# Reordering the expert loop, spreading the weight folding and pacing the last scatters in a fused graph and mixture-of-experts kernel on Trainium2

## The chip, the cores and the metric

The kernel runs on one core of one Trainium2 chip. The metric is the device time in microseconds (us) of one execution, as the median of several runs. Engines are named as in the profile: PE (TensorE) with PEld (its weight loads), DVE (VectorE), ACT (ScalarE), POOL (GpSimd) and SP (SyncE, which only issues DMAs here). A small `q` behind a name means its sequencer.

## The reference

The input is `x`, 128 graphs of 128 nodes with 128 features, in float32, and a weighted adjacency matrix for each. Four residual layers follow each other:

```
x = x + gnn0(layernorm(x), adj)       # softmax-like attention over neighbours
x = x + ffn0(layernorm(x))            # 30 steps of tanh, silu, layernorm, 128x128 product
x = x + relu(z @ Wa + (adj @ z) @ Wb + bias)     # z = layernorm(x), second graph layer
logits = x @ Wr + br                  # for each of 16384 tokens, 8 experts
top 2 experts, weights w1, w2 from the softmax
out = x + sum_k w_k * (gelu((norm(x)*g_e + b_e) @ W1[e] + b1[e]) @ W2[e] + b2[e])
```

W1[e] is 128x512 and W2[e] 512x128. Only the two chosen experts of a token count.

## The kernel before

The 128 graphs are 16 streams of 8. All engines run their own programs, written out by hand, and meet in semaphores; there is no scheduler. So the order on an engine is the order of the calls in its block, and each wait stands in the code ahead of the instruction that it holds.

**The second graph layer** is a pipeline over `GNN1_SLOTS` steps. In step k stream k is transposed, stream k-1 multiplied, k-2 mixed with its adjacency, k-3 finished on VectorE (`finish_rows`, `row_variances`), k-4 given its logits, k-5 routed (`route`), k-6 ranked (a matmul that counts tokens of each pair of experts), k-7 placed (`find_slots`). Placing gives each token a row in `sorted_rows`, in DRAM. There are 28 pairs of experts, each with a region of its own, and a token with its two weights, its index, its mean and variance is one row of 133 floats. POOL writes the rows by eight indirect DMAs a stream (`scatter`, L538), four ahead of the power operation for a later stream and four behind it. After step 15 there is no such operation, and the last four streams' 32 scatters stand directly one behind the other.

**Folding.** The layer norm's scale and shift of each expert are folded into W1 and its bias, after the pipeline's streams: TensorE sums the columns (`fold_wide`) and adds `b1` by a 1-row matmul (L1206, L1208), VectorE combines (L833). The eight experts go by twos in the last steps, from step 19.

**Between the stages.** VectorE turns the pairs' row counts into tables: which 128 rows (a slab) are to be loaded, and for which two experts (`slab_row`, `slab_exp`). Regions are rounded up to slabs, so SP and ACT fill 29 pieces of padding (`fill`, L376), waiting for `tables_ready`. Then SP copies eight weight matrices and loads the first rows (`load_weights` L423, `load_rows` L416), after `w1_folded`, `pads_in` and `scattered`.

**Experts.** 156 slabs of 128 tokens, each with two experts. The first 12 and the last 12 slabs are unrolled, 132 run in a loop of 12 a turn. Products are numbered o, two a slab. POOL computes the row scales (`scale`, L569) and writes results by an indirect DMA (`store`, L574). VectorE normalizes rows (`normalize`, L896), adds the second bias from `b2_all` by the expert's number, and combines (`finish`, L904, L909). ACT does the GELU (L1022) and copies the transposed rows (L1027). TensorE's order for an even o is:

```python
first_product(i, o)
if o % 2 == 0 and (not end or o < 2 * EACH - 4):
    turn(i, o // 2 + 2)
if not first or o >= 2:
    second_product(i, o - 2, expert_of(i, o - 2))
```

`turn` (L1225) transposes the rows of the slab after next and waits for its `normalize`. `expert_of` (L1221) loads the expert's number from SBUF into a register; `second_product` (L1244) picks its weights by it. `first_product` (L1235) reads one of eight buffers `w1_in_use`, which SP fills again once `hidden_psum` shows that the product of eight before is done.

## Time and profile before

| what | us |
|---|---|
| median of 3 runs (2808.33 to 2822.69) | 2814.98 |
| the profiled execution, its own time | 2804.9 |
| its span, first to last instruction | 2803.1 |
| PE busy in the span | 2489.5 |
| DVE busy | 2075.3 |
| POOL busy | 2029.8 |
| ACT busy | 1809.0 |

The profile is that of one execution, which was 10 us shorter than the median. A busy time is a sum over stages that differ. Where a stage is bound is read from the waits inside it and from the starts of neighbouring instructions. A row names the tile that lies at an address first, so `adjT` and `resid` also stand for the buffers of the expert stage that lie over them.

### The profile page before, as it was taken

The numbers are of one execution on the slowest core, as the hardware profiler recorded it, in microseconds if no ns is written. First come the engines' busy times: TensorE is split into PE (matmuls) and PEld (weight loads), VectorE is DVE, ScalarE is ACT, GpSimd is POOL, SyncE is SP. The second block draws the span as 40 slices with busy tenths as digits, with TensorE's granted clock in tenths as the row PEclk, the third lists the DMA queues.
The fourth block names the chain that finished last, engine by engine and source line by source line (L and its number), as shares of the span: only waits on it lengthen the run. The fifth ranks groups of instructions, "written<-read, shape, count | busy, mean of one in ns | idle before, by whom it ended". The sixth has DMA issues, their size and how long they took to land.

```text
span 2803.1 us, 62675 instructions
## 1 busy us (share of the span) xinstructions
PE 2489.5 (89%) x19950; PEld 2340.0 (83%) x19951; DVE 2075.3 (74%) x5754; ACT 1809.0 (65%) x2185; POOL 2029.8 (72%) x1592
## 2 busy tenths in 40 slices
PE   6839999999999999999999999886588888888887
PEld 5839999999999999999999999882577777777777
DVE  6999999999999999999999998674122222222222
ACT  3779999999999999999999973220222222222222
POOL 5779999999999999999999997775232332323323
PEclk9969999999999999999999999995799999999999
DMA  9000000000000000000000000411433333333332
GB/s 267 35 1 1 0 0 0 0 0 0 0 0 0 0 0 0 0 0 0 0 0 0 0 1 32 132 43 49 141 129 125 123 125 125 127 123 126 123 123 76
DMA packets 123642, 141.98 MB, mean 51 GB/s; under 512 B 14951, under 2 KB 76547, under 8 KB 123553
## 3 DMA queue, kind: packets, MB, share of 16 engines
q1 hardware_dynamic: 112450, 122.86, 13.3%
q0 software_dynamic: 9088, 17.14, 1.9%
q10 hardware_dynamic: 2016, 0.95, 0.1%
q8 instruction: 37, 0.61, 0.1%
q14 instruction: 51, 0.42, 0.0%
HBM read 36.35 MB, written 24.58 MB: 22 GB/s over the span
## 4 chain that ended last, share of the span: by engine, by line
DVE 54%; PE 29%; issue 9%; ACT 4%; another core or an unknown queue 2%; SPq 1%; DMA 0%; DVEq 0%; POOL 0%; POOLq 0%; ACTq 0%
DVE pair_stats L639 23%; DVE state L682 17%; PE psum L1244 12%; PE psum L1235 10%; DVE state L661 6%; PE psum L1072 3%; ACT adjT L1022 3%; PE psum L1062 2%; DVE it_vars L643 1%; DVE x_stats L639 1%; DVE resid L709 1%; DVE state L678 1%; DVE resid L669 0%; PE psum L1208 0%
## 5 line engine op out<-in xcount | busy, mean ns | idle before, releaser
L1072 PEld LDWEIGHTS psum<-w_ffn,turned 128*128 128x128 f32 x7680 | 1010.0, 192 | 36.1
L1072 PE MATMUL psum<-w_ffn,turned 128*128 128x128 f32 x7680 | 1013.6, 275 | 0.0
L495 POOL TENSOR_TENSOR it_rstd<-it_vars,minus_half 128x8 f32<-128x8 f32 x480 | 786.3, 1638 | 0.0
L498 POOL TENSOR_TENSOR state<-state,it_rstd 128x768 f32<-128x768 f32 x480 | 708.8, 1477 | 37.7
L639 DVE BATCH_NORM_STATS2 pair_stats<-state 128x6 f32<-128x256 f32 x1920 | 684.9, 417 | 0.0
L1062 PE MATMUL psum<-ident,state 128*128 128x128 f32 x4352 | 596.7, 281 | 72.3 <-DVE state L678 43.0
L574 POOL DMA_INDIRECT out_dram<-resid,adjT x156 | 161.3, 1034 | 554.5 <-DVE resid L909 544.1
L682 DVE SCALAR_TENSOR_TENSOR state<-state,psum 128x1024 f32<-128x1024 f32 x464 | 560.7, 1208 | 1.3 <-ACT state L943 0.7
L1022 ACT ACTIVATE adjT<-psum 128x512 f32<-128x512 f32 x312 | 186.4, 597 | 578.5 <-PE psum L1235 578.4
L1062 PEld LDWEIGHTS psum<-ident,state 128*128 128x128 f32 x4352 | 478.2, 143 | 90.8 <-issue 69.5
L936 ACT COPY turned<-psum 128x1024 f32<-128x1024 f32 x480 | 485.9, 1012 | 78.5 <-PE psum L1062 41.9
L946 ACT ACTIVATE state<-state 128x1024 f32<-128x1024 f32 x480 | 512.7, 1068 | 29.5 <-DVE state L678 9.1
L904 DVE TENSOR_TENSOR resid<-psum,resid 128x128 f32<-128x128 f32 x312 | 91.1, 292 | 543.7 <-PE psum L1244 543.3
L943 ACT ACTIVATE state<-psum 128x1024 f32<-128x1024 f32 x464 | 481.0, 1037 | 0.0
L1244 PE MATMUL psum<-resid,adjT 128*128 x2496 | 352.9, 284 | 109.9 <-ACT adjT L1022 109.9
L1244 PEld LDWEIGHTS psum<-resid,adjT 128*128 128x128 f32 x2496 | 302.1, 191 | 140.2 <-issue 138.3
L1068 PE MATMUL psum<-bias_mv,ones_bf 128*128 128x512 bf16 x992 | 377.8, 381 | 0.2 <-DVE state L757 0.2
L1235 PE MATMUL psum<-resid,adjT 128*128 128x128 f32 x2496 | 332.2, 276 | 0.0
L661 DVE TENSOR_SCALAR state<-state,it_rstd 128x128 f32<-128x128 f32 x960 | 319.7, 373 | 0.0
L1235 PEld LDWEIGHTS psum<-resid,adjT 128*128 128x128 f32 x2496 | 305.4, 193 | 1.2
L538 POOL DMA_INDIRECT sorted_rows<-state,slot x128 | 124.7, 974 | 53.7 <-issue 40.2
L909 DVE SCALAR_TENSOR_TENSOR resid<-resid,adjT 128x128 f32<-128x128 f32 x312 | 109.7, 352 | 23.1 <-DVE resid L904 2.9
(192 smaller groups left out, 1710.0 us busy)
## 6 DMA issues: line engine op xcount, KB each, us to landing
adjT<-resid SPq DMA_DIRECT2D x312, 256.0 KB, 2.3
adjT<-sorted_rows SPq DMA_DIRECT2D x156, 66.5 KB
resid<-in_x_dram SPq DMA_DIRECT2D x16, 512.0 KB, 7.3
state<-in_adj_dram SPq DMA_DIRECT2D x16, 512.0 KB, 7.3
adjT_dram<-adjT SPq DMA_DIRECT2D x7, 512.0 KB, 3.7
adjT<-adjT_dram SPq DMA_DIRECT2D x7, 512.0 KB, 3.5
out_dram<-resid,adjT POOLq DMA_INDIRECT x156, 2.5
sorted_rows<-state,slot POOLq DMA_INDIRECT x128
```

Source lines behind the costliest of these rows:

```text
L495: nc.gpsimd.tensor_tensor(it_rstd[s % 8][:, :], it_vars[s % 4][:, :], minus_half[:, 0:TILES], ALU.pow).then_inc(it_pow, 1)
L498: nc.gpsimd.tensor_tensor(values[s][:, 0:POOL_TILES, :], values[s][:, 0:POOL_TILES, :], wide(it_rstd[s % 8][:, 0:POOL_TILES]), ALU.mult).t ...
L639: last = nc.vector.bn_stats(dst[:, i, :], src[:, 2 * i:2 * i + 2, :].rearrange("p t d -> p d t"))
L661: last = nc.vector.tensor_scalar(values[r][:, t, :], values[r][:, t, :], it_rstd[r % 8][:, t:t + 1], None, ALU.mult)
L682: nc.vector.scalar_tensor_tensor(values[k], values[k], 0.01, ring[k % 4], ALU.mult, ALU.add).then_inc(state_read, 1)
L936: nc.scalar.copy(turned[s % 4], ring[s % 4]).then_inc(it_turned, 1)
L943: nc.scalar.activation(values[k], ring[k % 4], ACT.Tanh).then_inc(tanh_done, 1)
L946: nc.scalar.activation(values[v], values[v], ACT.Silu).then_inc(silu_done, 1)
L1062: last = nc.tensor.transpose(dst[:, t, :], src[:, t, :], ident[:, :])
L1072: last = nc.tensor.matmul(dst[:, t, :], stationary(t), moving(t), start=bias is None and m == 0, stop=m == len(terms) - 1, skip_group_chec ...
L1235: last = nc.tensor.matmul(psH[o % 4][:, c, :], w1[:, c * P:(c + 1) * P], turned_T[o // 2 % 4], start=True, stop=True)
L1244: last = nc.tensor.matmul(psY[o % 2], hidden[o % 4][:, c, :], w2_all[:, bass.ds(e, 1), c, :].rearrange("p o d -> p (o d)"), start=c == 0, ...
```

## The change

It has three parts.

**Experts.** On TensorE `turn` moves behind `second_product`; on VectorE `normalize` moves ahead of `finish`. The second bias is laid behind each expert's W1 (640 columns instead of 512) and comes with it, so VectorE no longer loads the expert's number, and a buffer of `w1_in_use` is free only once `y_biased` shows that the bias has been read. POOL computes scales six slabs ahead instead of four. SP copies four weights ahead of the first rows instead of eight, and the next four between them.

**Folding and fills.** Folding runs one expert a step from step 14 to 21, as one matmul and two VectorE operations (the scale, then `b1`, which is now loaded for all partitions, 2 MB). The pipeline has 23 steps instead of 24, and ranking comes last in a step. The padding is first written to DRAM (`pad_rows`) and filled from there in 16 pieces, once the pairs' ends are known (`ends_ready`): 10 fills on SP, 19 on ACT. The copies of token indices move to POOL's stretch before the pipeline.

**Scatters.** Where no power operation stands between, each four scatters wait until all before have landed.

```diff
@@ SP, experts @@
                 if u >= 8:
-                    sp.wait_ge(hidden_psum, u - 7)
+                    sp.wait_ge(y_biased, u - 7)
...
+            sp.wait_ge(pad_out, 16)
+            sp.wait_ge(ends_ready, 1)
+            for c in range(SP_FILLS):
+                fill(sp, c)
             sp.wait_ge(tables_ready, 1)
-            for c in range(0, PAIRS + 1, 2):
-                fill(sp, c)
             sp.wait_ge(w1_folded, NE)
-            for u in range(8):
+            sp.wait_ge(experts_in[2], 16)
+            for u in range(4):
                 load_weights(u)
             sp.wait_ge(pads_in, 16 * (PAIRS + 1))
             sp.wait_ge(scattered, 16 * STREAMS * TILES)
             for n in range(4 + AHEAD):
                 load_rows(n)
+                if n in (2, 3):
+                    load_weights(2 * n)
+                    load_weights(2 * n + 1)
@@ POOL, scatters of stream m, s is None in the last four steps @@
+                    if s is None:
+                        pool.wait_ge(scattered, 16 * TILES * m)
                     scatter(m, range(TILES // 2))
...
                 if m is not None:
+                    if s is None:
+
+                        pool.wait_ge(scattered, 16 * (TILES * m + TILES // 2))
                     scatter(m, range(TILES // 2, TILES))
@@ POOL, experts @@
-            for n in range(4):
+            for n in range(6):
                 scale(n)
             for n in range(SLABS):
-                if n + 4 < SLABS:
-                    scale(n + 4)
+                if n + 6 < SLABS:
+                    scale(n + 6)
                 store(n)
@@ DVE @@
+            def fold_weights(e):
+                dve.wait_ge(fold_psum, e + 1)
+                nc.vector.scalar_tensor_tensor(w1_all[:, e, 0:H], w1_all[:, e, 0:H], params[:, e, 0:1], psW,
+                                               ALU.mult, ALU.add).then_inc(w1_scaled, 1)
+                if e == 0:
+                    dve.wait_ge(experts_in[3], 16)
+                dve.wait_ge(w1_scaled, e + 1)
+                nc.vector.scalar_tensor_tensor(w1_all[:, e, 0:H], b1_all[:, e, :], 1.0 / D, w1_all[:, e, 0:H],
+                                               ALU.mult, ALU.add).then_inc(w1_folded, 1)
...
+                if 0 <= k - FOLD_FROM < NE:
+                    fold_weights(k - FOLD_FROM)
...
                 for x in range(2):
-                    e = expert_of(i, o, x)
                     dve.wait_ge(y_psum, i * (2 * EACH) + (2 * o + x + 1))
-                    nc.vector.tensor_tensor(y_sum[x], psY[x], b2_all[:, bass.ds(e, 1), :].rearrange("p o d -> p (o d)"),
-                                            ALU.add).then_inc(y_biased, 1)
+                    nc.vector.tensor_tensor(y_sum[x], psY[x], w1_in_use[(2 * o + x) % 8][:, H:WB], ALU.add
+                                            ).then_inc(y_biased, 1)
...
                 for o in range(EACH):
+                    if not end or o < EACH - 3:
+                        normalize(i, o + 3)
                     if not first or o >= 1:
                         finish(i, o - 1, not first or o >= 5)
-                    if not end or o < EACH - 3:
-                        normalize(i, o + 3)
@@ PE, experts @@
                     first_product(i, o)
+                    if not first or o >= 2:
+                        second_product(i, o - 2, expert_of(i, o - 2))
                     if o % 2 == 0 and (not end or o < 2 * EACH - 4):
                         turn(i, o // 2 + 2)
-                    if not first or o >= 2:
-                        second_product(i, o - 2, expert_of(i, o - 2))
```

How the instructions stand, first on TensorE in the loop of the experts, from an even first product to the next second product, before:

```order
L1235 MATMUL psum<-resid,adjT 128x128 [waits hidden_ready,slab_turned,w1_in6]
L1235 MATMUL psum<-resid,adjT 128x128 x3
L1224 REGISTER_ALU
L1225 MATMUL psum<-ident,resid 128x128 [waits rows_normed]
L1221 ISA
L1221 TENSOR_LOAD slab_exp
L1221 ISA x2
L1240 REGISTER_ALU
L1244 ISA [waits y_biased,hidden_ready]
L1244 MATMUL psum<-resid,adjT 128x128
```

The same place after the change (L1256 is the first product, L1265 the second, L1246 the transpose; seven rows, which are the second product's further ISA and MATMUL pairs, stand between the two fences):

```order
L1256 MATMUL psum<-resid,adjT 128x128 [waits hidden_ready,slab_turned,w1_in6]
L1256 MATMUL psum<-resid,adjT 128x128 x3
L1242 ISA
L1242 TENSOR_LOAD slab_exp
L1242 ISA x2
L1261 REGISTER_ALU
L1265 ISA [waits y_biased,hidden_ready]
L1265 MATMUL psum<-resid,adjT 128x128
```

```order
L1265 MATMUL psum<-resid,adjT 128x128
L1245 REGISTER_ALU
L1246 MATMUL psum<-ident,resid 128x128 [waits rows_normed]
L1256 MATMUL psum<-resid,adjT 128x128 [waits hidden_ready,w1_in7]
L1256 MATMUL psum<-resid,adjT 128x128 x3
```

The register load, which stood behind the transpose and its wait, now stands directly behind the four matmuls of a first product, and the transpose is followed by the odd first product.

On POOL, the last scatters before the scales of the experts, before and after:

```order
L538 DMA sorted_rows<-state,slot 462464x133 x7
L538 DMA sorted_rows<-state,slot 462464x133 [waits slots_ready,columns_ready,x3_pow]
L538 DMA sorted_rows<-state,slot 462464x133 x7
L569 TENSOR_TENSOR row_scale<-adjT,minus_half 128x1 [waits slab_in0]
```

```order
L556 DMA sorted_rows<-state,slot 462464x133 [waits slots_ready,scattered,columns_ready,x3_pow]
L556 DMA sorted_rows<-state,slot 462464x133 x3
L556 DMA sorted_rows<-state,slot 462464x133 [waits scattered]
L556 DMA sorted_rows<-state,slot 462464x133 x3
L591 TENSOR_TENSOR row_scale<-adjT,minus_half 128x1 [waits slab_in0]
```

Eight scatters in a row have become two fours with a wait on `scattered` each.

## Rows read from the trace of the kernel before

**Rows 1.** The page, part 1, whole span: busy us (share of span) xinstructions.

```profile
PE 2489.5 (89%) x19950; PEld 2340.0 (83%) x19951; DVE 2075.3 (74%) x5754; ACT 1809.0 (65%) x2185; POOL 2029.8 (72%) x1592
```

**Rows 2.** Stretches: length, each engine busy (x), granted TensorE clock, DMA share, GB/s.

```profile
1700.00:1952.00 252.00, 210.93 (x1532) 181.28 (x1532) 166.00 (x625) 54.31 (x82) 183.64 (x178) 0.85 0.22 69
...
1988.00:2803.10 815.10, 660.95 (x5147) 600.48 (x5147) 240.85 (x779) 226.68 (x468) 250.40 (x310) 1.00 0.35 121
```

**Rows 3.** Waits, 1990 to 2803: who <- whom: us in total, times, longest.

```profile
PE psum L1244 <- ACT adjT L1022: 109.9, 152, 0.9
...
PE psum L1225 <- DVE resid L896: 36.5, 142, 0.4
...
SPq L423 <- PE psum L1235: 252.2, 151, 2.2
```

**Rows 4.** Timeline, TensorE, one slab: start, us, line, out<-in, xcount [idle before <-releaser].

```profile
2103.30 1.06 PE L1235 MATMUL psum<-resid,adjT 128*128 128x128 f32 x8
2104.61 0.33 PE L1225 MATMUL psum<-ident,resid 128*128 128x128 f32 x1 [0.26 <-DVE resid L896]
2105.68 1.15 PE L1244 MATMUL psum<-resid,adjT 128*128 x8 [0.73 <-ACT adjT L1022]
2106.66 1.06 PE L1235 MATMUL psum<-resid,adjT 128*128 128x128 f32 x8
2107.56 0.36 PE L1244 MATMUL psum<-resid,adjT 128*128 x1
```

**Rows 5.** Timeline, TensorE, first product of the stage, and a transpose followed by one.

```profile
1988.33 1.06 PE L1235 MATMUL psum<-resid,adjT 128*128 128x128 f32 x4
...
1990.03 0.42 PE L1225 MATMUL psum<-ident,resid 128*128 128x128 f32 x1
1990.24 1.06 PE L1235 MATMUL psum<-resid,adjT 128*128 128x128 f32 x4
```

**Rows 6.** One line in one stretch: xcount: ns min/median/max, first and last start.

```profile
L1225 PE MATMUL psum<-ident,resid x132: 327/329/332, 2057.4 to 2743.3; 128*128 128x128 f32 x132
...
L1225 PE MATMUL psum<-ident,resid x10: 328/329/332, 1997.0 to 2041.6; 128*128 128x128 f32 x10
...
L1221 PEldq TENSOR_LOAD <-slab_exp x264: 296/312/637, 2057.4 to 2744.7; - x132
```

**Rows 7.** Timeline, SP's queue, between routing and experts.

```profile
1957.89 15.20 SPq L376 DMA_DIRECT2D sorted_rows<-pad  x15
1973.80 9.33 SPq L423 DMA_DIRECT2D adjT<-resid  x8
1983.97 6.98 SPq L416 DMA_DIRECT2D adjT<-sorted_rows  x7
```

**Rows 8.** Timeline, POOL, the last scatters (32 from 1906.21 on).

```profile
1904.94 0.96 POOL L538 DMA_INDIRECT sorted_rows<-state,slot  x1 [0.31 <-issue]
1906.21 0.96 POOL L538 DMA_INDIRECT sorted_rows<-state,slot  x1 [0.30 <-issue]
...
1951.45 0.96 POOL L538 DMA_INDIRECT sorted_rows<-state,slot  x1 [0.31 <-issue]
```

**Rows 9.** Scatters 1861 to 1953; landing in sorted_rows; weight copies (KB, us to landing).

```profile
L538 POOL DMA_INDIRECT sorted_rows<-state,slot x60: 956/962/1057, 1863.6 to 1951.5; - x60
...
DMA to landing us min/median/max: 1.9/2.5/2.9
...
adjT<-resid SPq DMA_DIRECT2D x304, 256.0 KB, 2.3
```

**Rows 10.** Timeline, VectorE, in find_slots of streams 14 and 15.

```profile
1927.17 0.39 DVE L808 TENSOR_TENSOR place<-psum,pair_end 128x224 f32<-128x224 f32 x1 [11.41 <-remote]
...
1932.65 0.17 DVE L813 CAST slot<-rank 128x8 int32<-128x8 f32 x1
```

**Rows 11.** The fold: VectorE operation and 1-row matmul, ns min/median/max.

```profile
L833 DVE SCALAR_TENSOR_TENSOR resid<-resid,params,psum x8: 742/747/748, 1912.5 to 1946.3; 128x512 f32<-128x512 f32 x8
...
L1208 PE MATMUL psum<-resid,frac x16: 1052/1135/1217, 1907.1 to 1945.2; 1*128 1x512 f32 x16
```

More of the change, by code:

```diff
@@ L88, in network @@
         psL = psum[:, 6, 0:TILES * NE].rearrange("p (t e) -> p t e", e=NE)
-        psR = psum[:, 7, 0:(TILES + 1) * PAIRS].rearrange("p (t e) -> p t e", e=PAIRS)
-        psW = [psum[:, 2 + j, :] for j in range(2)]
+        psR = psum[:, 6, 2 * P:2 * P + (TILES + 1) * PAIRS].rearrange("p (t e) -> p t e", e=PAIRS)
+        psW = psum[:, 7, :]
         psT = [psum[:, j, 0:3 * P].rearrange("p (v j) -> p v j", v=3) for j in range(2)]
@@ L207, in network @@
         y_sum = [over_resid(15, 1)[:, D * (6 + j):D * (7 + j)] for j in range(2)]
-        row_scale = [sb(f"row_scale{j}", [P, 1]) for j in range(4)]
+        w1_in_use = [over_adjT(0, 5)[:, WB * q:WB * (q + 1)] for q in range(8)]
+        hidden = [by_tile(over_adjT(5, 2)[:, H * j:H * (j + 1)], HC) for j in range(4)]
+        rows_in = [over_adjT(7, 2)[:, ROW * q:ROW * (q + 1)] for q in range(EACH)]
+        row_scale = [sb(f"row_scale{j}", [P, 1]) for j in range(EACH)]
         psX = [psum[:, j, 0:SLAB] for j in range(2)]
@@ L367, in stages, with by_queue @@
                     yield base + j, j % STREAMS
+        def by_queue(rows):
+            return rows.rearrange("r c -> (r c)").rearrange("(q n) -> q n", q=16)
         def fill(queue, c):
@@ L375, in fill @@
                 dst = sorted_rows[PAIRS * REGION:PAIRS * REGION + SLAB, :]
-            queue.dma_start(dst, pad[:, :].bitcast(F32)).then_inc(pads_in, 16)
+            queue.dma_start(by_queue(dst), by_queue(pad_rows)).then_inc(pads_in, 16)
+        SP_FILLS = 10
         @block.sync
@@ L1011, in _ @@
                     nc.scalar.copy(turned[3], psF).then_inc(r_turned, 1)
-            act.wait_ge(tables_ready, 1)
-            for c in range(1, PAIRS + 1, 2):
+            act.wait_ge(pad_out, 16)
+            act.wait_ge(ends_ready, 1)
+            for c in range(SP_FILLS, PAIRS + 1):
                 fill(act, c)
@@ L1134, in _, with fold_sums @@
             iteration(STEPS, tail=True)
+            def fold_sums(e):
+                if e == 0:
+                    pe.wait_ge(fold_ready, 1)
+                    pe.wait_ge(experts_in[0], 16)
+                else:
+                    pe.wait_ge(w1_scaled, e)
+                nc.tensor.matmul(psW, fold_wide[:, e, :], w1_all[:, e, 0:H], start=True, stop=True).then_inc(fold_psum, 1)
             for k in range(GNN1_SLOTS):
                 a, b, f, d, h = in_flight(k, 0, Q_LAG, ROWS_LAG, MIX_LAG, RANK_LAG)
-                if h is not None:
-                    pe.wait_ge(hot_ready, h + 1)
-                    if h >= 1:
-                        pe.wait_ge(place_step, (h - 1) * PLACE_STEPS + 4)
-                    picks = hot[h % 4][:, :, :]
-                    nc.tensor.matmul(psR[:, 0:TILES, :], tri[:, :], picks, start=True, stop=False, skip_group_check=True)
-                    for t in range(TILES):
-                        rest = TILES - t
-                        last = nc.tensor.matmul(psR[:, t + 1:TILES + 1, :], ones_bf[:, :],
-                                                picks[:, t, :].unsqueeze(1).to_broadcast([P, rest, PAIRS]),
-                                                start=False, stop=t == TILES - 1, skip_group_check=True)
-                    last.then_inc(rank_psum, 1)
                 if a is not None:
@@ L1195, in _ @@
                     last.then_inc(logit_psum, 1)
[L1196 to L1209 removed]
+                if h is not None:
+                    pe.wait_ge(hot_ready, h + 1)
+                    if h >= 1:
+                        pe.wait_ge(place_step, (h - 1) * PLACE_STEPS + 4)
+                    pe.wait_ge(route_step, ROUTE_STEPS * min(k - ROUTE_LAG, STREAMS - 1) + 1)
+                    picks = hot[h % 4][:, :, :]
+                    nc.tensor.matmul(psR[:, 0:TILES, :], tri[:, :], picks, start=True, stop=False, skip_group_check=True)
+                    for t in range(TILES):
+                        rest = TILES - t
+                        last = nc.tensor.matmul(psR[:, t + 1:TILES + 1, :], ones_bf[:, :],
+                                                picks[:, t, :].unsqueeze(1).to_broadcast([P, rest, PAIRS]),
+                                                start=False, stop=t == TILES - 1, skip_group_check=True)
+                    last.then_inc(rank_psum, 1)
+                if 0 <= k - FOLD_FROM < NE:
+                    fold_sums(k - FOLD_FROM)
             pe.wait_ge(diag_ready, 1)
```

79 lines of the change are left out of this document (29 added, 50 removed).

## The prediction

> **What bounds the kernel now.** I read the page's totals first, then the span cut into its stages, then in each stage what ends the waits. TensorE is busy 89% of the span [rows 1], but that is an average over unlike stages. The cut [rows 2] shows what follows the first 1700 us (first layer and FFN iterations, where no edit falls): 252 us of the second graph layer and routing, then from 1952 to 1988 a bridge of 36 us, and 815 us of experts, where PE is busy 661 us at a granted clock of 1.00 and no other engine more than 250 us. The experts are 29% of the time and hold 154 us of idle TensorE.
>
> The waits of that stage [rows 3] say where they are: 109.9 us before the second product and 36.5 us before the transpose, both of TensorE. The timeline of one slab [rows 4] is the one to learn from. A product's eight matmul records start 0.90 us (2106.66 to 2107.56) to 0.98 us (2105.68 to 2106.66) before the next product's. But from the even first product (2103.30) to the transpose (2104.61) there are 1.31 us, and from the transpose to the second product (2105.68) 1.07 us, where a transpose followed directly by a product takes 0.21 us (1990.03 to 1990.24) [rows 5]. The view blames ScalarE for the second gap, yet the GELU it names belongs to a later product. What stands between is the sequencer's own work: the load of the expert's number from `slab_exp` (312 ns median [rows 6]), register steps and two waits. After the odd first product the same load stands too, and costs no gap (2106.66 to 2107.56 is 0.90 us): the queued matmuls cover it. The first gap is real: the transpose waits for `normalize`, which VectorE runs only behind `finish` of an older slab.
>
> The period: 132 transposes in the loop, the first at 2057.4 and the last at 2743.3 us [rows 6], so 685.9/131 = 5.24 us a slab. In the unrolled slabs ten run from 1997.0 to 2041.6, 44.6/9 = 4.96 us.
>
> The 36 us before are a chain: the last folds (L833, to 1946.3 [rows 11]), tables, then on SP 15 pad fills in 15.2 us, 8 weight copies in 9.3 us and the first rows at 1983.97 [rows 7]; the first product starts at 1988.33 [rows 5]. The scatters, on POOL, had been issued by 1951.45 [rows 8].
>
> **The change part by part.**
>
> *Experts on TensorE and VectorE.* The transpose goes behind the second product, and `normalize` ahead of `finish`. The register load now follows a first product in both halves, and the rows of a transpose are ready a whole slab before. So 1.31 us falls to 0.90 and 1.07 to 0.21: 1.27 us less, 3.97. I don't take all of it: the half that already has this form takes 0.98 + 0.90 = 1.88 us [rows 4], two of them 3.76, and the transpose 0.21, 3.97 again; its register step and the even half's extra wait I put at 0.08 more, since the sequencer, not the array, seems to pace this half. Forecast 4.05 us in the loop, 3.9 unrolled. 132 x (5.24 - 4.05) = 157 us and 24 x (4.96 - 3.9) = 25 us: **182 us less**. Bounds: 3.8 us if only the array counts (4 x 0.90 + 0.21; 33 us more gain), 4.5 if 0.45 of the 1.27 us stays (59 us less gain).
>
> Does anything else need over 4.05 us? SP: its 5.24 us hold 252.2/156 = 1.62 us of waiting [rows 3], so 3.6 us of work; weights with the bias behind them (320 KB for 256) may add 0.1. That is close under, and it works ahead through eight buffers. DMA: a share of 0.35 of 5.24 us is 1.8 us [rows 2]; with weights a quarter larger about 2.3. VectorE 241/156 = 1.5 us, and it loses two register loads a slab; ScalarE 1.5, POOL 1.6. A weight buffer is now held until `finish` has read the bias, one slab longer; eight buffers are four slabs, 16 us, against a landing of 2.3 us [rows 9] and one slab of delay: hidden. POOL computes scales six slabs ahead, ahead of the store: the rows for that are issued three slabs ahead by SP, so the store can be some 0.5 us late; four output buffers cover it.
>
> *Waits in the scatters.* The last 32 scatters go out 1.27 us apart (1904.94, 1906.21) [rows 8], so they queue without a pause. Now each four wait until all before have landed. Landing takes 1.9 to 2.9 us, median 2.5 [rows 9]; with 0.2 us for the wait to pass, each of 8 waits costs 2.7 - 1.27 = 1.4 us, 11 us in all, and it is POOL alone that stands behind it. Bounds: 8 x 0.7 and 8 x 1.9, 6 and 15 us. The Trainium skill, page "DMA: Bandwidth & Descriptors", section "Anatomy of one DMA — SWDGE (gpsimd) path", fits a DMA from this engine as 2.0 us and its bytes at 436 GB/s, 2.2 us for 68 KB; by it the waits would cost an estimated 9 us.
> The new chain: first wait ends 1904.94 + 2.7 = 1907.6; seven halves of 3 x 1.27 + 2.7 = 6.5 us; the last half 3.8 + 2.5; all landed at 1959.4. Beside the old chain VectorE stood idle 11.41 us up to 1927.17 [rows 10], while scatters ran back to back. No instruction shown explains it; a pause each 6.5 us may shorten it, which I don't count.
>
> *Folding spread out.* Eight folds go from the tail into steps 14 to 21, on VectorE two operations each: 2 x 0.747 [rows 11] + 0.1 = 1.6 us, 13 us, less 0.7 for one moved. Five or six of them fall where VectorE is without idle time, so `find_slots` of stream 15 moves from 1932.7 [rows 10], which has the 11.41 us stall in it, to about 1928. The chain needs it at 1945 for the last scatters. On TensorE the 1-row matmul goes (16 records, median 1.14 us) [rows 11]. The cover is those 17 us; gone, each us of folding counts.
> The new fold reads two SBUF operands. The Trainium skill, page "SBUF — State Buffer", section "SBUF: two separate sides", says that such a VectorE operation and a GpSimd operation that reads SBUF lock each other out. By the page it would be up to an estimated 8 x 0.75 = 6 us. The scatters were 956 to 1057 ns long beside VectorE operations of that kind (as L810, place times hot, in every step) [rows 9], so my sum takes zero.
>
> *Fills and loads.* Fills start once the pair ends are known (about 1929), 19 on ScalarE's queue at 1.0 us: done 1949, landed 1951.5. SP: 10 fills and 4 weight copies at 1.17 us, done by 1944. Both lie beside the scatters. So after 1959.4 only the register read (0.7) and 1983.97 to 1988.33, 4.4 us, remain: experts begin at **1965, 23 us earlier**. The 2 MB bias load and the later copies of weights lie beside POOL's pace; I allow 2 us, bounds -2 and +10. The token copies (16 x 0.2 us) move on POOL to a stretch ahead of its later idle time: 0.
>
> **Sum.** 182 + 23 - 2 = 203 us. The profiled execution took 2804.9 us, so 2602; the median before is 2815, 10 above it, and against it I forecast **2612 us**.
>
> **The rivals.**
> A, the sum as above, 2575 to 2640: 0.74.
> B, the register load comes out from cover. The sequencer must get ahead of the array in both halves; if it doesn't, about 0.45 us a slab stay: 4.5 us, 2612 + 59 = 2671, up to 2730. For it: in the good half there is almost no slack. Against: 312 ns loads beside 0.89 us of queued matmuls. The Trainium skill, page "Runtime: NRT & Kernel Launch", section "The launch sequence", gives such a load about 1.3 us from HBM. By it the load and its 0.6 us of steps would overrun the 0.9 us of cover by an estimated 1.0 us a half. The 0.90 us of [rows 4] excludes that here. Chance 0.14.
> C, the experts stay at 5.2 us because feeding them binds (SP or landings), and only the start is gained: 2815 - 21 = 2794. Against: SP waits 1.6 us of each slab now. 0.06.
> D, slower: the ring finish, SP's row load, `scale`, store. POOL's store of slab n stands behind the scale of slab n+6, whose rows SP issues only after `finish` of n-1, and `finish` of n+4 waits for the store to land. That path is now about 1.2 + 1.1 + 2.5 + 0.6 + 1.0 + 2.5 = 9 us over five slabs. It decides from 5 x 5.24 = 26 us; at 28 us the slab takes 5.6 us, 48 us more, less 21: 2842. 0.04.
> No effect within 0.5% (the edits cancel): 0.02.
>
> **How the numbers follow.** The likeliest case gives 2612. The range 2575 to 2690 holds A and half of B, 0.8; C, D and B's far part lie outside. About 0.5% is what a measurement can tell from no change. Faster A + B + C 0.94, the same 0.02, slower 0.04.
>
> **What would show it.** The transposes of the loop 4.0 to 4.1 us apart; TensorE's idle before the second product near 0; the waits of ScalarE and VectorE still on TensorE; SP waiting under 0.6 us a slab; the last 32 scatters in fours with pauses of about 1.7 us where 0.3 stood, the last issued at about 1957, the first product at 1965. Wrong if the period is above 4.3, if SP or a landing ends TensorE's waits, or if fills or folds still run when the scatters have landed.

## The result and the profile after

| | us |
|---|---|
| changed kernel, median of 4 runs (2563.86 to 2566.49) | 2565.14 |
| kernel before, beside it, median of 4 runs | 2812.61 |
| ratio, 95% interval | 0.912 (0.909 to 0.914) |
| profiled execution after, and its span | 2566.49, 2564.7 |

247 us less where 203 were forecast. The time is 47 us under the forecast and 10 us below the range.

Part 1 of the page, to be held against [rows 1]:

```profile
PE 2378.7 (93%) x19678; PEld 2320.6 (90%) x19935; DVE 2081.9 (81%) x5761; ACT 1811.9 (71%) x2185; POOL 2027.5 (79%) x1592
```

The span cut at the first product of the experts, columns as in [rows 2]:

```profile
1700.00:1979.10 279.10, 200.15 (x1503) 186.35 (x1518) 174.35 (x639) 55.04 (x83) 184.11 (x173) 0.82 0.26 83
1979.10:2564.70 585.60, 576.98 (x5147) 576.25 (x5146) 241.92 (x778) 230.40 (x468) 249.19 (x310) 1.00 0.57 205
```

In this cut is the whole account. The experts take 585.6 us where they took 815.1 from 1988 on: 229.5 less. They begin at 1979.2 where they began at 1988.3: 9 less. Together 238 us, the difference of the two spans (2803.1 and 2564.7). The other 9 of the 247 come from the two profiled executions: that of before was 8 us under its median, that of after 1 over. TensorE is busy 577 of the 585.6 us, so it is now the bound; before it was busy 661 of 815. That the busy time itself fell by 84 us for the same 5147 records is not less work. A record alone counts in full (1.06 us for a product [rows 4]), while back to back the next one starts 0.89 us after it and covers its end; and records behind a wait were longer (a transpose 329 ns [rows 6], now 273).

The waits of the stage, 1990 to the end, as in [rows 3]:

```profile
ACT adjT L1044 <- PE psum L1256: 260.0, 276, 1.3
DVE resid L925 <- PE psum L1265: 209.2, 194, 1.3
POOL row_scale L591 <- DMA adjT<-sorted_rows: 192.4, 144, 3.1
```

And those of SP's queue:

```profile
SPq L434 <- DVE resid L925: 1.7, 3, 0.7
```

Both lines in which TensorE waited (109.9 and 36.5 us) are gone; everything else waits for it. SP waited 252.2 us for a weight buffer [rows 3], now 1.7. It is no longer ahead of TensorE but level with it, and GpSimd waits for rows that land later than they did.

TensorE, one slab, columns as in [rows 4]:

```profile
2101.55 0.27 PE L1246 MATMUL psum<-ident,resid 128*128 128x128 f32 x1
2101.66 1.06 PE L1256 MATMUL psum<-resid,adjT 128*128 128x128 f32 x8
2102.55 1.06 PE L1265 MATMUL psum<-resid,adjT 128*128 x8
2103.44 1.06 PE L1256 MATMUL psum<-resid,adjT 128*128 128x128 f32 x8
2104.34 1.06 PE L1265 MATMUL psum<-resid,adjT 128*128 x8
2105.23 0.27 PE L1246 MATMUL psum<-ident,resid 128*128 128x128 f32 x1
```

No row has an idle time. Each product follows the last by 0.89 us and the transpose is followed by a product after 0.11 us: 4 x 0.89 + 0.11 = 3.67 us, and 3.68 between the two transposes. All transposes from 2040 to 2520, one line:

```profile
L1246 PE MATMUL psum<-ident,resid x130: 272/273/273, 2041.7 to 2517.7; 128*128 128x128 f32 x130
```

476.0/129 = 3.69 us a slab. The forecast was 4.05, with 3.8 as its lower bound.

Between the stages, SP's queue, to be held against [rows 7]:

```profile
1938.15 12.74 SPq L384 DMA_DIRECT2D sorted_rows<-pad_rows  x10
1951.97 4.71 SPq L434 DMA_DIRECT2D adjT<-resid  x4
1974.81 2.60 SPq L427 DMA_DIRECT2D adjT<-sorted_rows  x3
```

And GpSimd's last scatters, the first of some of the fours, and the last of all, against [rows 8]:

```profile
1916.11 0.95 POOL L556 DMA_INDIRECT sorted_rows<-state,slot  x1 [2.15 <-DMA sorted_rows<-state,slot]
...
1929.64 0.95 POOL L556 DMA_INDIRECT sorted_rows<-state,slot  x1 [2.14 <-DMA sorted_rows<-state,slot]
...
1943.99 0.96 POOL L556 DMA_INDIRECT sorted_rows<-state,slot  x1 [3.10 <-DMA sorted_rows<-state,slot]
...
1961.56 0.95 POOL L556 DMA_INDIRECT sorted_rows<-state,slot  x1 [3.07 <-DMA sorted_rows<-state,slot]
...
1971.72 0.96 POOL L556 DMA_INDIRECT sorted_rows<-state,slot  x1 [0.30 <-issue]
```

SP has its weights by 1956.7 and then stands until 1974.8, when the last scatter has landed: the scatters are now the chain's end, as forecast, but the last is issued at 1971.7, not 1957.

### The profile page after: what moved, and what is told of

The parts are those of the page before. It is cut to its first block, busy times and chain, and to the rows that moved or that the text cites. A ratio compares the mean times of both kernels' runs of the same rounds, so it can differ in the third digit from the quotient of the medians.

```text
span 2564.7 us, 60894 instructions
## 1 busy us (share of the span) xinstructions
PE 2378.7 (93%) x19678; PEld 2320.6 (90%) x19935; DVE 2081.9 (81%) x5761; ACT 1811.9 (71%) x2185; POOL 2027.5 (79%) x1592
## 4 chain that ended last, share of the span: by engine, by line
DVE 58%; PE 31%; issue 7%; POOL 1%; DMA 1%; ACT 1%; SPq 1%; another core or an unknown queue 0%; DVEq 0%; POOLq 0%; ACTq 0%
DVE pair_stats L661 25%; DVE state L704 18%; PE psum L1265 11%; PE psum L1256 11%; DVE state L683 6%; PE psum L1094 5%; PE psum L1084 2%; DVE it_vars L665 2%; DVE x_stats L661 1%; POOL sorted_rows L556 1%; DVE resid L731 1%; PE psum L1213 1%; DMA sorted_rows<-state,slot 1%; PE psum L1246 1%; DVE state L700 1%
## 5 line engine op out<-in xcount | busy, mean ns | idle before, releaser
L957 ACT COPY turned<-psum 128x1024 f32<-128x1024 f32 x480 | 485.8, 1012 | 80.4 <-PE psum L1084 43.9
L925 DVE TENSOR_TENSOR resid<-psum,adjT 128x128 f32<-128x128 f32 x312 | 91.0, 292 | 305.1 <-PE psum L1265 209.2
L1265 PE MATMUL psum<-resid,adjT 128*128 x2496 | 330.0, 275 | 2.0 <-DVE resid L925 2.0
L1256 PE MATMUL psum<-resid,adjT 128*128 128x128 f32 x2496 | 330.9, 276 | 0.0
L1265 PEld LDWEIGHTS psum<-resid,adjT 128*128 128x128 f32 x2496 | 303.6, 192 | 2.6 <-issue 2.4
L1256 PEld LDWEIGHTS psum<-resid,adjT 128*128 128x128 f32 x2496 | 304.8, 193 | 0.0
L1090 PE MATMUL psum<-bias_mv,ones_bf 128*128 128x512 bf16 x736 | 279.7, 380 | 0.0
L591 POOL TENSOR_TENSOR row_scale<-adjT,minus_half 128x1 f32<-128x1 f32 x156 | 89.3, 572 | 208.6 <-DMA adjT<-sorted_rows 205.5
```

Of the source, the lines that this page charges most:

```text
L957: nc.scalar.copy(turned[s % 4], ring[s % 4]).then_inc(it_turned, 1)
L1256: last = nc.tensor.matmul(psH[o % 4][:, c, :], w1[:, c * P:(c + 1) * P], turned_T[o // 2 % 4], start=True, stop=True)
L1265: last = nc.tensor.matmul(psY[o % 2], hidden[o % 4][:, c, :], w2_all[:, bass.ds(e, 1), c, :].rearrange("p o d -> p (o d)"), start=c == 0, ...
```

## The experiments

Fifteen runs in four groups, each group on one chip beside the kernel before. The chips were of two kinds, which matters for the start of the experts: on two of them the kernel before takes 2778 us (e1 to e4, e8 to e11), on the other two 2811 to 2816 (e5 to e7, e12 to e15). In microseconds only kernels of one group are compared, across groups the ratios.

### Which edit shortens the slab

The question is whether the 1.5 us a slab come from TensorE's order, VectorE's order, or both. e1 leaves both and only loads the expert's number ahead of the transpose, in the kernel before:

```diff
                     first_product(i, o)
+                    e = expert_of(i, o - 2) if not first or o >= 2 else None
...
-                        second_product(i, o - 2, expert_of(i, o - 2))
+                        second_product(i, o - 2, e)
```

> The kernel before, with one edit on TensorE: the expert's number is loaded into its register ahead of the transpose instead of behind it. If the 1.07 us from transpose to second product is the exposed register load, it falls to 0.2 us or less and the loop's slab goes from 5.24 to 4.3 to 4.5 us, 110 to 140 us less in all (about 2690 us). If the gap is the wait for the GELU on ScalarE, as the view of waits says, nothing changes (2812 us).

Measured: 2654.8 us, ratio 0.956 (0.953 to 0.959); a slab is 4.41 us (100 transposes, 2060.9 to 2497.7). One piece of it on TensorE:

```profile
2103.58 1.06 PE L1235 MATMUL psum<-resid,adjT 128*128 128x128 f32 x8
2104.90 0.33 PE L1225 MATMUL psum<-ident,resid 128*128 128x128 f32 x1 [0.26 <-DVE resid L896]
2105.20 1.04 PE L1244 MATMUL psum<-resid,adjT 128*128 x7
```

From the transpose to the second product it is 0.30 us where it was 1.07 [rows 4], so the register load in the open did cost 0.77 us a slab, as the prediction read it. The wait for `normalize` (1.32 us from product to transpose) stays.

e2 moves only the transpose behind the second product on TensorE, e3 moves only `normalize` ahead of `finish` on VectorE, e4 does both; nothing else is changed in any of them.

```diff
@@ e2, TensorE @@
-                    if o % 2 == 0 and (not end or o < 2 * EACH - 4):
-                        turn(i, o // 2 + 2)
                     if not first or o >= 2:
                         second_product(i, o - 2, expert_of(i, o - 2))
+                    if o % 2 == 0 and (not end or o < 2 * EACH - 4):
+                        turn(i, o // 2 + 2)
@@ e3, VectorE @@
+                    if not end or o < EACH - 3:
+                        normalize(i, o + 3)
                     if not first or o >= 1:
                         finish(i, o - 1, not first or o >= 5)
-                    if not end or o < EACH - 3:
-                        normalize(i, o + 3)
```

> The kernel before, with the transpose behind the second product on TensorE, VectorE's order left. Theory array: the order on TensorE alone is enough, since the transpose then has 0.9 us more for its rows; the slab takes 4 x 0.89 + 0.11 = 3.7 us in the loop as after the whole change, some 225 us less (about 2585 us). Theory both: without normalize ahead of finish the transpose still waits; the slab takes 4.0 us or more (2630 us or more).

> The kernel before, with normalize ahead of finish on VectorE, TensorE's order left. The transpose no longer waits: 1.31 us from the even first product to the transpose falls to 0.9, the 1.07 us behind it stays. The slab takes about 4.8 us, 60 us less (about 2750 us). If the two gaps are one wait that only moves, nothing changes.

> The kernel before with both orders, and nothing else of the change (bias still picked by register on VectorE, fills, folds and scatters as before). If the two orders are all that matters in the experts, the loop's slab takes 3.68 us as after, and the time is 2812 - 225 = about 2585 us. If the bias carried with the weights or the scales six slabs ahead are needed too, the slab stays above 3.8 us (2600 us or more).

| | us | ratio (interval) | us a slab |
|---|---|---|---|
| e2, TensorE's order | 2552.4 | 0.919 (0.916 to 0.922) | 3.72 |
| e3, VectorE's order | 2847.0 | 1.025 (1.022 to 1.028) | 5.73 |
| e4, both | 2845.2 | 1.024 (1.021 to 1.027) | 5.70 |

One moved line gives nearly the whole gain, and the second makes the kernel slower than before. In e4 the wait that does it, 2060 to 2500:

```profile
POOL out_dram L574 <- DVE resid L909: 312.5, 77, 4.3
DVE resid L896 <- POOL row_scale L569: 193.2, 77, 2.5
```

Every `normalize` waits 2.5 us for its scale. The timeline of e4, GpSimd and VectorE, shows the circle:

```profile
2101.88 1.03 POOL L574 DMA_INDIRECT out_dram<-resid,adjT  x1 [4.13 <-DVE resid L909]
...
2102.95 0.58 POOL L569 TENSOR_TENSOR row_scale<-adjT,minus_half 128x1 f32<-128x1 f32 x1
...
2103.56 0.35 DVE L896 TENSOR_SCALAR resid<-adjT,row_scale 128x128 f32<-128x128 f32 x1 [2.51 <-POOL row_scale L569]
...
2104.51 0.29 DVE L904 TENSOR_TENSOR resid<-psum,resid 128x128 f32<-128x128 f32 x1 [0.60 <-issue]
...
2106.13 0.29 DVE L904 TENSOR_TENSOR resid<-psum,resid 128x128 f32<-128x128 f32 x1 [0.87 <-issue]
...
2106.45 0.35 DVE L909 SCALAR_TENSOR_TENSOR resid<-resid,adjT 128x128 f32<-128x128 f32 x1
```

GpSimd's scale for four slabs on stands behind its store, the store waits for `finish`, `finish` now stands behind a `normalize`, and that waits for the scale. Two engines hand each other one token a slab, and the period is that of the round trip. If so, the change's third edit, scales six ahead, is what breaks the circle. Three kernels ask that.

e8 is e4 with that edit (and a `row_scale` for each slab of the ring); e9 is the changed kernel without it:

```diff
@@ e8, on e4 @@
-                if n >= 4:
-                    pool.wait_ge(rows_normed, n - 3)
+                if n >= EACH:
+                    pool.wait_ge(rows_normed, n - EACH + 1)
...
-            for n in range(4):
+            for n in range(6):
                 scale(n)
             for n in range(SLABS):
-                if n + 4 < SLABS:
-                    scale(n + 4)
+                if n + 6 < SLABS:
+                    scale(n + 6)
                 store(n)
@@ e9, on the changed kernel @@
-            for n in range(6):
+            for n in range(4):
                 scale(n)
             for n in range(SLABS):
-                if n + 6 < SLABS:
-                    scale(n + 6)
+                if n + 4 < SLABS:
+                    scale(n + 4)
```

> The kernel before with both new orders (TensorE's transpose behind the second product, VectorE's normalization ahead of the finish) and, new against e4, GpSimd's scales six slabs ahead with a row_scale buffer for each slab of the ring. Theory ring (what made e3 and e4 slow is that a scale four ahead stands behind the store of the slab before on GpSimd, which waits for the finish, which in this order waits for a normalization that waits for the scale): the wait of VectorE for row_scale, 2.5 us a slab in e4, is gone, a slab takes 3.7 us, and the time is about 0.92 of the kernel before. Rival copies (the finish's register loads and the bias read out of b2_all make VectorE too slow in this order): the slab stays over 4.5 us, the time at 0.95 or above.

> The changed kernel with GpSimd's scales only four slabs ahead of the store, all else as changed. Theory ring: VectorE's normalization waits for row_scale again, since scale n+4 stands behind store n-1; without the register loads of the finish the round trip is some 1.2 us shorter than e4's 5.7, so 4.3 to 4.7 us a slab and 2650 to 2720 us. Rival copies: without the register loads nothing waits, 3.7 us a slab and 2566 us.

e8: 2545.9 us, ratio 0.917 (0.914 to 0.919), 3.69 us a slab (119 transposes, 2062.8 to 2497.8). From 1.024 to 0.917 by two scales more in advance. e9: 2619.4 us, 0.943 (0.940 to 0.946), 4.14 us a slab; in its view of waits, 2060 to 2500:

```profile
DVE resid L918 <- POOL row_scale L591: 269.1, 106, 5.2
POOL out_dram L596 <- DVE resid L930: 259.3, 105, 4.0
```

So the circle is shown from both sides. Its size in e9 I had too high (4.3 to 4.7): from `normalize` to the first bias sum it takes 0.27 us there and 0.95 in e4, and to the second 0.92 where e4 takes 2.57; `finish` without its register loads is the faster part of the circle.

e11 asks whether VectorE's order is needed at all: the changed kernel with `finish` first, as before (e3's diff backwards).

> The changed kernel with VectorE's old order in the expert loop: finish of slab n-1 ahead of the normalization for slab n+3. Theory array (TensorE's order alone sets the slab): 3.7 us a slab, and the time within 5 us of 2565. Rival both (the normalization has to come first, since the transpose now follows the products): the slab is over 3.8 us, the time over 2580.

2552.7 us, 0.919 (0.916 to 0.922), 3.71 us a slab. It isn't needed: e2, e8 and e11 have slabs of 3.72, 3.69 and 3.71. The order of TensorE alone sets them, and with that order `normalize` is in time either way. The bias behind W1 gains nothing here either: e8 still loads the expert's number on VectorE. It only makes the circle shorter where there is one (4.14 in e9 against 5.70 in e4).

### How close SP is

```diff
+                at = sp.value_load(slab_row[0:1, n:n + 1], min_val=0, max_val=PAIRS * REGION)
                 at = sp.value_load(slab_row[0:1, n:n + 1], min_val=0, max_val=PAIRS * REGION)
```

> The changed kernel with one more register load for each slab on SyncE (the row's address read twice). Theory edge (SyncE issues a slab in 3.60 us, TensorE computes one in 3.68): a load of 0.3 to 0.6 us puts SyncE's own period at 3.9 to 4.2, the slab follows it, and the time rises by 30 to 70 us, to 2595 to 2635. Rival slack (SyncE waits for y_biased or y_stored for more than 0.3 us a slab in places that the view of waits does not name): the slab stays at 3.7 and the time within 5 us of the changed kernel's.

2671.2 us, 0.962 (0.959 to 0.964). SP's queue in e10:

```profile
2104.32 0.34 SPq L428 DMA_DIRECT2D adjT<-sorted_rows  x1
2105.38 1.67 SPq L435 DMA_DIRECT2D adjT<-resid  x2
2108.76 0.34 SPq L428 DMA_DIRECT2D adjT<-sorted_rows  x1
```

and in the changed kernel, in a stretch in which SP catches up:

```profile
2103.07 1.68 SPq L434 DMA_DIRECT2D adjT<-resid  x2
...
2106.68 1.68 SPq L434 DMA_DIRECT2D adjT<-resid  x2
...
2110.28 1.68 SPq L434 DMA_DIRECT2D adjT<-resid  x2
```

SP needs 3.60 us a slab, TensorE 3.68. One more register load with its steps took 4.43 - 3.60 = 0.83 us, more than the 0.3 to 0.6 I had expected, and the slab followed to 4.48 us (98 transposes, 2061.1 to 2495.8): theory edge, with a dearer load. In the changed kernel SP is only 0.08 us a slab from being the bound.

### Where the start of the experts was lost

e5 takes the eight waits out of the changed kernel, e6 puts the fold's matmul at the head of TensorE's step instead of behind the ranking, and e7 lets the fills wait for `tables_ready`, as before the change.

```diff
@@ e5 (the same at 16 * (TILES * m + TILES // 2)) @@
-                    if s is None:
-                        pool.wait_ge(scattered, 16 * TILES * m)
@@ e6, TensorE, first in the step instead of last @@
+                if 0 <= k - FOLD_FROM < NE:
+                    fold_sums(k - FOLD_FROM)
@@ e7, SP, ahead of the fills @@
             sp.wait_ge(ends_ready, 1)
+            sp.wait_ge(tables_ready, 1)
@@ e7, ACT, ahead of the fills @@
-            act.wait_ge(ends_ready, 1)
+            act.wait_ge(tables_ready, 1)
```

> The changed kernel without the eight waits on landed scatters. Theory cost: POOL's last 32 scatters are the path, 8 waits of 1.2 to 2 us come off, the last scatter is issued near 1958 instead of 1971.7 and the kernel is 8 to 14 us faster than with the waits (about 2554 us). Theory relief: run back to back the scatters hold up TensorE and VectorE (before, VectorE stood idle 11.4 us beside them), the last placements come late, and the time is the same within 3 us or up to 6 us longer.

> The changed kernel with each fold's matmul at the head of its step on TensorE instead of the end. VectorE waits 1.5 to 3.5 us for it in each of steps 15 to 19, and that made the placements and so the last scatters some 8 us late. If so, those waits vanish, the last scatter is issued 6 to 10 us earlier and the kernel is 5 to 9 us faster (about 2558 us). If POOL alone sets the pace there, nothing changes.

> The changed kernel with the fills started only when the tables are ready, 7 to 8 us later. If they have slack beside the scatters (ScalarE's 19 fills end at 1961, the last scatter lands at about 1974), the time is the same within 3 us; fills end near 1969. If fills slow the landings of scatters by sharing the DMA engines (waits of 3.1 us instead of 1.6 to 2.1 while they run), the same number of slow waits moves later, and the time again stays. Over 5 us slower would mean that fills are on the path.

On one chip: e5 2570.6 (2569.5 to 2573.7), e6 2562.0 (2561.3 to 2564.2), e7 2565.6 (2563.2 to 2567.2). e7's ratio is 0.911, that of the changed kernel 0.912, so starting the fills early gains nothing. e5 loses 5 us on e7, in ranges that do not overlap. Its last scatter goes out at about 1957, 15 us sooner than in the changed kernel, but now the fills are the end of the chain:

```profile
1942.47 24.98 SPq L384 DMA_DIRECT2D sorted_rows<-pad_rows  x10
1942.42 33.53 ACTq L384 DMA_DIRECT2D sorted_rows<-pad_rows  x19
...
1962.55 13.41 ACTq L384 DMA_DIRECT2D sorted_rows<-pad_rows  x12
```

They start 4 us later than in the changed kernel: VectorE had stood idle for 6.2 us ahead of the pairs' ends (below). And they take longer: 10 on SP in 25 us where the changed kernel takes 12.7, 19 on ACT in 33.5 where it takes 23.0. The third line shows that the last 12 on ACT, behind the scatters, take 1.1 us each; the 7 before them stand for the most part among scatters and take the other 20 us. The first transpose stands at 1981.5.

e6's median is 3.6 us under e7's, the ranges just overlap, and 5 to 9 were expected. In the changed kernel VectorE had waited seven times for `fold_psum` (3.54, 1.46, 3.05, 3.09, 2.45, 0.71 and 1.92 us, 16.2 in all). In e6 it no longer does, but it waits for the ranks instead. The two waits in the changed kernel, 1700 to 1960, and the one that is left in e6:

```profile
DVE place L830 <- PE psum L1225: 13.9, 4, 7.2
DVE resid L839 <- PE psum L1165: 13.2, 6, 3.5
...
DVE place L830 <- PE psum L1227: 23.8, 8, 7.3
```

So most of the wait only moved: the first scatter behind a wait starts at 1914.2 in e6 and at 1915.2 in e7, the last at 1969.8 and 1970.9.

Then the whole on one chip again. e12 is the changed kernel, e13 is e8 once more (the new expert loop with everything ahead of it as before), e14 is e13 with only the eight waits added, e15 is e6 without the last four of the eight.

```diff
@@ e14, on e13 @@
                     pool.wait_ge(slots_ready, m + 1)
+                    if s is None:
+                        pool.wait_ge(scattered, 16 * TILES * m)
...
+                    if s is None:
+                        pool.wait_ge(scattered, 16 * (TILES * m + TILES // 2))
@@ e15, on e6, at both waits @@
-                    if s is None:
+                    if s is None and m < STREAMS - 2:
```

> The changed kernel itself once more, beside the next three on one chip. Its slab stays at 3.7 us everywhere. Where the chip is one on which the kernel before takes 2778 us, its first transpose should stand near 1963 as e11's did, and it ends at 2549 to 2553; where it takes 2812, near 1978 and at 2565.

> The kernel of e8 once more: the three new orders of the expert loop with everything ahead of it as before. Theory start (the change's new order of routing, folds and fills is worth what the start of the experts moved on the slower chip, 9 to 14 us): slower than the changed kernel by 9 to 14 us on a chip of the 2812 kind. Rival no start (the gain at the start was the chip's and the execution's, the new order ahead of the experts brings nothing): within 3 us of the changed kernel or faster, as on the 2778 chip, where e8 was 6.8 us faster than e11.

> The kernel of e13 with only the eight waits between the halves of the last four scatters added. Theory relief (with scatters back to back the releases that TensorE sends to VectorE come late, 11.4 us once; a wait between the halves lets them through): on a chip of the 2812 kind the idle times of VectorE that end remotely are gone and it is 5 to 20 us faster than e13; on the other kind, where e8 shows no such idle time, it is 5 to 12 us slower, by the eight landings. Rival tax: 5 to 12 us slower on either.

> e6 (fold matmul at the head of each step) without the last four of the eight waits, where VectorE no longer waits for TensorE's ranks. Theory room: the last scatters end 4 to 6 us earlier beside the fills, which take longer for it, and the whole gains 0 to 4 us on e6, 3 to 8 on the changed kernel. Rival collision (as in e5, the fills take twice as long beside scatters back to back): it loses up to 6 us against the changed kernel.

| | us (lowest to highest) | ratio (interval) | first transpose | idle ended remotely, 1700 to 1960 |
|---|---|---|---|---|
| e12, changed | 2566.9 (2564.6 to 2568.1) | 0.913 (0.911 to 0.914) | 1979.8 | 33 us |
| e13, old order ahead | 2583.9 (2581.4 to 2590.2) | 0.920 (0.918 to 0.921) | 1994.9 | 107 us |
| e14, and the waits | 2571.7 (2567.9 to 2580.0) | 0.914 (0.913 to 0.916) | 1992.7 | 94 us |
| e15, half free | 2556.4 (2554.3 to 2559.8) | 0.909 (0.908 to 0.911) | 1968.2 | 31 us |

e13 against e12: everything that the change does ahead of the experts is worth 17 us on this chip, and the start of the experts moved by 15. e14 against e13: the waits alone give 12 of the 17. On such a chip that is theory relief in its sign, by runs that do not overlap. Its trace shows only part of it (2 us at the start); the profiled execution was e14's slowest, 2580.0.

The last column is the sum of the waits that end in "remote", for which the trace has no instruction. In e13:

```profile
ACT turned L1000 <- remote: 37.9, 4, 10.7
DVE state L757 <- remote: 37.1, 5, 11.0
```

and in the changed kernel's first trace:

```profile
DVE place L830 <- remote: 15.4, 2, 8.1
```

Most of this column is no evidence on the eight waits, since it lies ahead of them: e13 and e14 are the same program up to the last four streams, and all of e14's 94 us end by 1894.3. What counts is the stretch in which the waits act. The rows for e13 from 1912 to 1960:

```profile
DVE resid L833 <- remote: 6.8, 2, 6.1
DVE place L808 <- remote: 4.7, 2, 4.5
```

That is 11.5 us. Before the change it is 11.9 there (the 11.41 of [rows 10] among them) and in e5 6.2. In the changed kernel, e6, e7, e12, e14 and e15, all with pauses (e15 with four), there is not one such row. So on these chips the two go together in nine traces: without pauses VectorE is held up beside the last scatters, with them it is not.

In the traces of the eight kernels on the 2778 chips there is not one such wait; the seven on the 2812 chips have 28 to 107 us of them, and the first traces of before and after 74 and 29. e13 and e8 are the same code: 2583.9 and 2545.9 us, first transpose at 1994.9 and 1960.5. On the faster kind the old order ahead of the experts is no loss at all: e8 is 6.8 us faster than e11. What the eight waits alone do on such a chip was not run.

e15 is 10.5 us faster than the changed kernel on its chip, with intervals that don't meet: theory room, and more than the 3 to 8 expected. It beats both kernels. In the traces its last scatter is issued at 1961.4 (e12: 1973.7) and its first transpose comes 11.6 us sooner. Whether its gain over e6 is from the four waits is less sure, since the two ran on different chips and their ratios to the kernel before are equal (0.909 both); e6 against e7 was 3.6 us, e15 against e12 10.5.

## Why the prediction was wrong

**What bounds the kernel: right.** The idle TensorE of the experts, at its two places, was the gain. e1 priced the register load at 0.77 us a slab.

**The expert term: right mechanism, mis-sized.** Two steps of it failed, both too careful. "The transpose 0.21" was read at 1990.03 to 1990.24 [rows 5], where the clock was granted at half. The stretches of the kernel before around it:

```profile
1988.00:1990.00 2.00, 1.94 (x9) 1.95 (x10) 0.44 (x3) 1.41 (x2) 1.08 (x2) 0.50 0.28 68
1990.00:1992.00 2.00, 2.00 (x12) 2.00 (x11) 0.26 (x1) 0.91 (x3) 0.54 (x1) 0.51 0.25 68
1992.00:1996.00 4.00, 4.00 (x38) 4.00 (x38) 0.68 (x3) 1.96 (x4) 0.00 (x0) 1.00 0.44 153
```

0.50 and 0.51 are the lower level, 1.2 GHz, after a bridge in which TensorE was busy 5.3 of 38 us; from 1992 it is the full one (1.00), and there a transpose and the product behind it stand 0.11 us apart:

```profile
1992.85 0.27 PE L1225 MATMUL psum<-ident,resid 128*128 128x128 f32 x1
1992.96 1.06 PE L1244 MATMUL psum<-resid,adjT 128*128 x8
```

And "0.98 + 0.90", the half "that already has this form", followed a stall of 0.73 us [rows 4]. The 0.98 belongs to it: a product right behind a wait has that pitch elsewhere too (0.99 in e1, 2105.20 to 2106.19; 0.99 after the change behind the one wait of 2.02 us, 1989.17 to 1990.16), and products without a wait take 0.89. Why a wait makes the next product slower is not shown. The 0.08 put on top "since the sequencer seems to pace this half" was not there. So 4.05 became 3.68, and the range's own bound, 3.8, was built on the same 0.21. At 3.68 the term is 132 x 1.56 + 24 x 1.28 = 237 us; 229.5 were measured. The 7 us are in the unrolled slabs: outside the 132 the stage took 815.1 - 691.7 = 123.4 us before and 585.6 - 485.8 = 99.8 after, 23.6 less and not 31; the 4.96 us had been read from ten of the first slabs and taken for all 24. "Normalize ahead of finish" was credited as the other half of the cause; e2 and e11 show that it was not needed, and e3 and e4 that with scales only four ahead it makes the kernel 2.5% slower.

**Who else needs more than the slab: right, narrowly.** SP's 3.6 us were right (3.60), the 0.1 for longer weights was not there.

**The start, 23 us earlier: wrong, 9 measured, 15 in the pair e13 and e12.** The last scatters end the chain, as forecast, but SP could load the first rows only at 1974.8, where 1959.4 had been given for the landing. Two terms failed.

The first wait was put at 1907.6; it ended at 1916.1. The scatter ahead of it was 8.1 us late (1913.0 for 1904.9), a lateness that the sum had put at nothing. 3.4 us of it stand already at the very first scatter, long before any fold: 1754.79 where it was 1751.40. There VectorE stood for the rank, which TensorE now does last in its step, and the kernel before had no such wait:

```profile
1752.14 0.39 DVE L830 TENSOR_TENSOR place<-psum,pair_end 128x224 f32<-128x224 f32 x1 [3.72 <-PE psum L1225]
```

Between e8 and e11 it is much the same, 3.8 us (1750.2 and 1754.0). No run moved the rank alone. The other 4.7 stay open. VectorE's waits for the fold's matmul, counted as none, are not shown to be the cause: e6 takes them out and the first wait ends only 1 us sooner than in e7, and on the faster chip, where e11 has 13.3 us of them too, the distance to e8 is still 2.9 us at 1889.3 and 1892.2.

"Seven halves of 6.5 us" were 7.4: from 1916.11 to 1967.93 there are seven, 51.8 us. The pauses ahead of the fours are 1.6 to 2.2 us, but 3.1 twice beside the fills, which makes 2.6 us more than the sum had. Another 3.4 are one stall of 3.70 us inside a four (1948.65), without a wait; the kernel before has such a one of 3.15 (1933.75), so it is not the change's. The forecast of the fills was off too (19 on ACT in 23 us from 1938, where 20 us from 1929 on had been given), but e7 shows that this cost nothing.

The two misses had opposite signs. The experts gave 47 us more than forecast and the start 12 less than its 21, so the time came out nearer to the range than the expert term alone would have put it. That is luck.

**Scatter waits as a cost of 11 us: wrong in sign on these chips.** The idle 11.41 us [rows 10] were seen and "not counted". It was gone after the change. e14 is 12 us faster with the waits and e5 5 us slower without, and idle time of this kind beside the last scatters is 11.5 us in e13, 6.2 in e5 and none in e14 and e12. GpSimd pays for the waits, 14.5 us by its eight pauses; the engines beside it gain. How a pause lets the releases through was not seen in a trace, so that part is argued. The Trainium skill's page "DMA: Bandwidth & Descriptors", section "Anatomy of one DMA — SWDGE (gpsimd) path", by which the waits cost an estimated 9 us, gave the same sign. For the pauses themselves the 1.1 us each of that estimate was low: six are 1.3 to 1.9 us longer than the 0.3 between other scatters, and two beside the fills 2.8.

**Rivals.** B (a load that comes out from cover): no, the 312 ns loads are as before and no gap shows them. C: no, SP needs 3.60 us and not the 5.2 that C needed; but TensorE's 3.68 is only 0.08 above it. D, the slower one: its ring (finish, SP's rows, scale, store) didn't close, but a shorter one between the same operations was 2.5% slower than the kernel before in e3 and e4, and with VectorE's new order only the edit "scales six ahead", which the prediction costed at nothing, keeps it open.

## What to carry to other kernels

Take a price per operation only from rows at the clock and in the queue state in which it will run: a pair of rows at half clock and a pitch just behind a stall together hid 0.37 us in 4.05. When two engines hand work to each other in turn, an order that looks harmless on one can close a circle over a short lead on the other; write down the lead (four scales, six scales) and walk the circle before costing the edit at nothing. A wait put into a queue of transfers is not only a cost: look at who is idle without a cause beside the queue. And judge an edit by the idle time of the stretch in which it acts: of e14's 94 us none lay behind its waits.

## What the runs showed of the hardware

- A register load on SP with its steps took 0.83 us of SP's time (e10); on TensorE the same kind of load costs nothing while matmuls are queued ahead of it, and 0.77 us where they are not (e1).
- On two of the four chips engines stood idle for 28 to 107 us between 1700 and 1960, the stretch with the indirect DMAs, with no instruction that ends the wait; on the other two never. e8 and e13 are one code and 38 us apart, their first transposes 34. Beside the last 32 scatters, VectorE has 6 to 12 us of it in the three traces without pauses there and none in the six with them. What holds the releases up, and why only on some chips, no run here tells.
- Copies within DRAM (the fills) on ACT's queue: in e5 the 7 that stood among indirect DMAs without a pause took 20 us, the 12 behind them 1.1 us each; with pauses between the DMAs, 19 took 23 us.
